# Where patch loads stand in the SyncE queue, and where GpSimd clears its buffers: one change to a fused token and transformer kernel

## What is computed

```python
pe   = conv(x, conv_w, stride 14)            # per image 9 x 9 patches, 256 channels
red  = mean of each 3 x 3 window of pe       # 9 windows per image
q    = ln(red) @ la_wq                       # 8 heads of 32
k, v = ln(window's 9 cells) @ la_wkv
agg  = softmax(q . k) weighted sum of v      # over the 9 cells of the window
lo   = red + agg @ la_proj_w + la_proj_b
patch_out = lo @ mod_w + mod_b               # 9 tokens
cls_out   = class attention over lo          # 1 token
h = concat(patch_out, cls_out, txt)          # 64 x 87 x 256
h = h + attention(ln(h))                     # 16 heads of 16, q and k normalised and rotated
h = h + ffn(ln(h))                           # linear + 2 of 8 low-rank experts
```

## Time and profile before

| | us |
|---|---|
| runs | 786.54, 795.9, 793.22 |
| median | 793.22 |
| the profiled execution's own time | 798.07 |
| its span, first to last instruction | 796.4 |

### The profile page before, as it was taken

The page is one execution under the profiler, slowest core; times in us unless marked ns, Lnnn a source line. Parts: engine busy times, 40 slices in busy tenths (PEclk is TensorE's granted clock), DMA queues, the critical chain, the costliest instruction groups (busy, mean ns, idle before and its releaser), DMA issues.

```text
span 796.4 us, 23804 instructions
## 1 busy us (share of the span) xinstructions
PE 708.1 (89%) x9335; PEld 564.9 (71%) x9335; DVE 547.5 (69%) x1208; ACT 408.2 (51%) x985; POOL 423.4 (53%) x450
## 2 busy tenths in 40 slices
PE   5998979987896388999899999999999999999974
PEld 4987757876673266887777777777777777877752
DVE  2377665873877556688677687887887887875641
ACT  4453423623433145666566556656557557666530
POOL 3577442652645726556447457566566566565211
PEclk9999969989897589999999999999999999999995
DMA  9940640704020121211221221222222222121100
GB/s 223 240 110 1 194 131 1 194 17 96 10 58 18 25 53 32 68 49 39 62 73 40 58 70 49 61 67 56 61 61 61 61 52 71 26 52 37 44 19 25
DMA packets 69524, 53.02 MB, mean 67 GB/s; under 512 B 36175, under 2 KB 68646, under 8 KB 69286
## 3 DMA queue, kind: packets, MB, share of 16 engines
q1 hardware_dynamic: 69414, 51.50, 25.9%
HBM read 33.69 MB, written 11.40 MB: 57 GB/s over the span
## 4 chain that ended last, share of the span: by engine, by line
PE 50%; DMA 13%; SPq 12%; DVE 11%; issue 5%; ACT 4%; POOL 4%; DVEq 0%; POOLq 0%; ACTq 0%
DMA out<-out_sb 8%; PE p_c L1305 8%; PE p_a L1305 7%; PE p_conv L764 6%; PE p_kv L764 6%; DMA xcols<-in_x_cols 5%; PE p_s L1366 4%; SPq L1060 4%; SPq L1061 4%; PE p_o L1375 3%; SPq L1050 2%; PE p_n L1383 2%; PE p_c L1423 2%; PE p_s L1348 2%; PE p_mm L764 2%
## 5 line engine op out<-in xcount | busy, mean ns | idle before, releaser
L1100 POOL TENSOR_TENSOR t<-t,ss_rs 116x512 f32<-116x512 f32 x48 | 51.0, 1062 | 152.8 <-ACT ss_rs L1149 152.8
L1243 DVE TENSOR_REDUCE mx<-p_s 87x16 bf16<-87x1392 f32 x64 | 102.2, 1597 | 8.9 <-PE p_s L1348 8.4
L1174 ACT ACTIVATE prT<-p_s 87x1392 f32<-87x1392 f32 x64 | 85.0, 1328 | 31.2 <-PE p_s L1366 31.2
L426 POOL TENSOR_TENSOR xs_lo<-xcols,xs_hi 120x585 fp32r<-120x585 f32 (+1 forms) x45 | 60.5, 1352 | 66.2 <-ACT xs_hi L489 66.2
L1096 POOL TENSOR_TENSOR t<-t 116x512 f32<-116x512 f32 x48 | 61.7, 1285 | 42.0 <-DVE t L1234 41.9
L1366 PE MATMUL p_s<-qr,kr 32*87 32x87 f32 x2048 | 68.6, 257 | 0.0
L1103 POOL TENSOR_TENSOR t<-t,tabs 116x512 f32<-116x512 f32 x48 | 61.1, 1273 | 1.5
L1305 PE MATMUL p_c<-w_f,yT 128*116 128x296 f32 x192 | 59.7, 436 | 1.7 <-ACT f L1199 0.6
L1366 PEld LDWEIGHTS p_s<-qr,kr 32*87 32x87 f32 x2048 | 60.1, 153 | 0.0
L1362 PE MATMUL p_s<-mxT,pick_row 32*87 32x87 bf16 x1024 | 55.7, 207 | 1.0 <-ACT mxT L1168 1.0
L1305 PE MATMUL p_c<-w_p,onT 128*116 128x256 f32 x192 | 54.3, 406 | 1.2 <-ACT yT L1193 0.9
(11 more groups left out here) (248 smaller groups left out, 1974.8 us busy)
## 6 DMA issues: line engine op xcount, KB each, us to landing
xcols<-in_x_cols SPq DMA_DIRECT2D x12, 822.7 KB, 11.8
h<-h_tokens SPq DMA_DIRECT2D x16, 348.0 KB
out<-out_sb SPq DMA_DIRECT2D x48, 116.0 KB
h_tokens<-in_txt SPq DMA_DIRECT2D x4, 1232.0 KB, 11.7
x<-in_txt_cols SPq DMA_DIRECT2D x32, 154.0 KB, 2.9
qr<-qkT SPq DMA_DIRECT2D x64, 58.0 KB, 2.0
kr<-qkT SPq DMA_DIRECT2D x64, 58.0 KB, 2.0
xcols<-in_x_cols SPq DMA_DIRECT2D x3, 759.4 KB, 13.5
```

The costliest lines, as they stand in the source:

```text
L426: nc.gpsimd.tensor_tensor(xs.lo[:, n % XS_SLOTS, :, 0:M].bitcast(F32R), raw, xs.hi[:, n % XS_SLOTS, :, 0:M], ALU.subtract).then_inc(S['xs_ ...
L1100: link(nc.gpsimd.tensor_tensor(t4, t4, ss_rs[:, b].unsqueeze(2).broadcast_to([TP, 2 * HEADS, HD]), ALU.mult))
L1174: nc.scalar.activation(prT[:, k % 2], p_s[0:SEQ, :, 0:QUADS * SEQ], ACT.Exp, scale=HD ** -0.5).then_inc(S['s_exp'], 1)
L1243: nc.vector.reduce_max(mx[:, k % 2, :, 0:QUADS], p_s[0:SEQ, :, 0:QUADS * SP].rearrange("p j (a k) -> p j a k", k=SP)[:, :, :, 0:SEQ], AX_X ...
```

## The change

Three edits. In SyncE's table `x.1` and `x.2` move from -64 and -30 to -317 and -245. In VectorE's table `sum.0` moves from 593 to 620. In GpSimd's code `clear()` is cut in two: the strips and `mx` are filled behind `xc` of group 1, `vp` behind the first `add` of group 0; the waits for the window stage's semaphores go with them.

```diff
--- before.py
+++ after.py
@@ -255,7 +255,7 @@
 WINDOW_DVE = table("""stats.0.-10 stats.1.48 xlo.0.55 stats.2.89 xlo.1.105 xlo.2.110 stats.3.147 xlo.3.162 xlo.4.172 stats.4.176
                 stats.5.183 stats.6.224 xlo.5.231 xlo.6.257 stats.7.304 stats.8.310 red_var.0.331 xlo.7.338
                 redb.0.342 xlo.8.375 q.0.380 q_kb.0.384 prod.0.400 score.0.427 prod.1.437 score.1.467 prod.2.477
-                score.2.498 s_max.0.517 att.0.538 sum.0.593 sum.1.638 lo.0.695 lo_var.0.700 patch.0.730 gv.0.752
+                score.2.498 s_max.0.517 att.0.538 sum.0.620 sum.1.638 lo.0.695 lo_var.0.700 patch.0.730 gv.0.752
                 g_m.0.774 g_att.0.818 gw.0.866 cls.0.960""")
 WINDOW_PE = table("""conv.0.-55 conv.1.-26 conv.2.6 xT.0.24 xT.1.41 conv.3.45 xT.2.63 conv.4.72 kv.0.90 xT.3.120 xT.4.122 conv.5.125
                 kv.1.143 kv.2.158 conv.6.172 xT.5.190 kv.3.193 conv.7.207 conv.8.225 xT.6.243 kv.4.246 kv.5.263
@@ -263,7 +263,7 @@
                 mod.0.718 patT.0.736 gv.0.738 gT.0.769 gB.0.850 ga.0.872 cl.0.910""")
 WINDOW_POOL = table("""xlo.0.-120 xlo.1.-71 xlo.2.-39 xlo.3.2 xlo.4.16 red.1.31 red.2.40 xlo.5.86 red.3.101 red.4.110 xlo.6.118
                 xlo.7.133 xlo.8.194 red.5.209 red.6.221 red.7.258 red.8.275 vw.0.551 vw.1.566 vw.2.582""")
-WINDOW_SP = table("""x.0.-398 x.1.-64 x.2.-30 rows.0.736 cls.0.970""")
+WINDOW_SP = table("""x.0.-398 x.1.-317 x.2.-245 rows.0.736 cls.0.970""")
 WINDOW_PERIOD = 403
 PIECES = CELLS // LOAD_CELLS
 X_SLOTS, XS_SLOTS, PE_SLOTS, XT_SLOTS, KV_SLOTS = 3, 3, 4, 3, 6
@@ -404,7 +404,7 @@
 
             return step
 
-        def gpsimd(pool, link, clear):
+        def gpsimd(pool, link):
             consts.fill_early(nc, pool, link)
             nc.gpsimd.memset(eps_q[:], 1e-5 * CELLS * CELLS * C).then_inc(S['fill'], 1)
 
@@ -449,12 +449,6 @@
                     if s == 0 and k == 2:
                         fill_pick()
                         consts.fill_late(nc, pool, link)
-                    if s == STEPS - 1 and k == 0:
-                        pool.wait_ge(S['conv'], CELLS * STEPS)
-                        pool.wait_ge(S['kv_mm'], CELLS * STEPS)
-                        pool.wait_ge(S['stat'], CELLS * STEPS)
-                        pool.wait_ge(S['red'], (CELLS - 1) * STEPS)
-                        clear()
 
             return step
 
@@ -1068,10 +1062,17 @@
         def gpsimd(pool, link):
             ready = counted(pool, S['set_0'])
 
-            def clear():
-
+            def clear_strips():
+
+                pool.wait_ge(W['conv'], CONVS)
                 for part in (qr, kr, mx):
                     ready(nc.gpsimd.memset(part[:], 0.0))
+
+            def clear_values():
+
+                pool.wait_ge(W['kv_mm'], CONVS)
+                pool.wait_ge(W['stat'], CONVS)
+                pool.wait_ge(W['red'], (CELLS - 1) * STEPS)
                 ready(nc.gpsimd.memset(vp[:, :, :, :, HD:], 1.0))
 
             def step(name, g, k):
@@ -1087,6 +1088,8 @@
                         "p c (b s) -> p c b s", b=GB))
                     nc.gpsimd.tensor_copy(images(x[:, half])[:, :, :, WINDOWS], consts.clsT[:, :, GB * g:GB * (g + 1)]
                                           ).then_inc(S['x_ok'], 1)
+                    if g == 1:
+                        clear_strips()
                 if name == 'xlo':
                     wait(pool, S['xhi'], g + 1)
                     nc.gpsimd.tensor_tensor(xT.lo[:, half].bitcast(F32R), x[:, half], xT.hi[:, half],
@@ -1094,6 +1097,8 @@
                 if name == 'add':
                     wait(pool, S['rot_ok'], 3 * g + k + 1)
                     link(nc.gpsimd.tensor_tensor(t1[:, b], t1[:, b], t2[:, b], ALU.add))
+                    if g == 0 and k == 0:
+                        clear_values()
                 if name == 'scale':
                     wait(pool, S['ss_rstd'], 3 * g + k + 1)
                     t4 = t1[:, b].rearrange("p (h d) -> p h d", d=HD)
@@ -1119,7 +1124,7 @@
                     link(nc.gpsimd.tensor_tensor(g_eq[:], g_eq[:], earlier[:].unsqueeze(1).broadcast_to(shape), ALU.mult))
                     nc.gpsimd.tensor_tensor(g_gt[:], g_gt[:], g_eq[:], ALU.add).then_inc(S['rank_in'], 1)
 
-            return step, clear
+            return step
 
         def scalar(act, link):
             def step(name, g, k):
@@ -1448,8 +1453,7 @@
         @block.gpsimd
         def _(pool):
             link = counted(pool, consts.S['pool_1'])
-            group_step, clear = groups[1](pool, link)
-            play(WINDOW_POOL, windows[1](pool, link, clear), GROUP_POOL, group_step)
+            play(WINDOW_POOL, windows[1](pool, link), GROUP_POOL, groups[1](pool, link))
 
         @block.scalar
         def _(act):
```

## The result

| | before | after |
|---|---|---|
| median of the timed runs, us | 790.55 (11 runs) | 767.94 (6 runs) |
| ratio, 95% interval | | 0.971 [0.966, 0.976] |
| profiled execution, us | 798.07 | 764.59 |
| its span, us | 796.4 | 762.9 |

The times are those of a second timing of both kernels, on one chip; the first gave 0.9705 [0.9628, 0.9783] with 767.93 us for the kernel after. So the gain is 22.9 us, with an interval from 19 to 27. A ratio leaves out the executions that ran slow (two of before and two of `sum_only` further down), a median takes all, so a gain worked out from a ratio can differ from the distance of two medians.

The account below looks back on a forecast made before the run. TensorE bounds the unchanged group stage, so the gain is in when that stage starts. Loads 10.5 us plus fills and sum 8.7 make 19.2, taking 793.2 to 774 us; range 765 to 785.

Parts of the forecast that it names:

- The fills and the sum: Between the stages: moved fills and `sum.0` behind `rotate.2` let `qk.0` of group 1 go 8.7 us earlier, bounds 7.8 to 9.4.
- `sum.0` within a microsecond behind `rotate.2`: Sign of being right, in the last step on VectorE: `sum.0` starts within a microsecond behind `rotate.2`.
- The third late load: Load `x.1` of step 4, at 187 us behind a row store: 9.2 us, from TensorE's 7.66 us wait plus 1.5 of clock.
- The rival by which it is shorter in other executions: Holes shorter in the timed runs: loads give 2.5 us, the whole 11.2, so 782 us; chance 0.12.
- The second late load: Load `x.1` of step 3, at 141 us behind a row store: 0.5 us, between 0 and ScalarE's idle 2.61.
- No such row of TensorE stands behind the second: Claim that no wait of TensorE follows the load at 141 us, though ScalarE sat idle 2.61 us.
- The share of 0.80 in 3.83: TensorE's wait against ScalarE's idle time at the load at 86 us, used to put the 141 us load at 0.5 us.
- The first late load: Load `x.1` of step 2, at 86 us behind a row store: 0.8 us, between nothing and ScalarE's 3.8.
- The cover "with only 0.2 us in hand": GpSimd's moved strips and `mx` fills end at 241.0 us, against 241.19 when the `add` begins, so they cost nothing.
- the first rival: Between the stages, fills slow VectorE or come late for `add.0`: 4.9 us lost, gain 14.3, so 779 us; chance 0.12.
- TensorE's clock as a loss: Rival: closer packed start keeps TensorE's clock low into the group stage; 30 us lost against 19 won, 804 us; chance 0.03.
- The first peak product some 19 us earlier: Sign of being right: the first peak product starts some 19 us earlier.

Follow-up runs that it names:

- `sum_only`: The kernel before with only `sum.0` put behind `rotate.2`, fills and loads as they were: ratio 0.9982, median 790.7 us.
- the kernel with copies: The kernel after with its two long GpSimd fills made by copies from one zero per partition: ratio 0.9671, 765.9 us.

## Why the prediction was nearly right

It said 774 us, 765 to 785; the time is 768, at the edge of the 768 to 778 that it gave its own working. The sum of 19.2 us came out as 22.9. Of the 6 us between 774 and 768 another 2.6 are luck of the starting point and no mechanism: the three runs of before that it started from had a median of 793.2, and with more runs it is 790.6. By the row stores, over all kernels, the terms 0.8, 0.5, 9.2 and 8.7 came out as 1.2, 4.8, 9.4 and 9.3, 24.7 together, inside the interval of the timed gain. So one term was wrong by far, and the total is near because the two large terms were right.

- **The fills and the sum, 8.7 us.** Measured 8.3 (5.1 to 11.5). The steps of that chain hold one by one: `sum.0` within a microsecond behind `rotate.2`, a wait for `qkT.1` of 4.76 us where about 5 were named, the bias held up by `add.2` (1.38 us), no product of VectorE over 2 us beside a fill.
- **The third late load, 9.2 us, 7.66 of wait and 1.5 of clock.** Measured by itself: 9.7 us by the row stores, 7.2 of wait and 2.3 of clock in its trace, 10.1 in the timed runs. The rival by which it is shorter in other executions falls: the 3rd row store stands 47.9 to 48.4 us ahead of the 4th in all four kernels with old loads.
- **The second late load, 0.5 us and at most 2.61: the step that failed.** It is worth 4.7 us by the row stores (3.2 by the median). "No such row of TensorE stands behind the second" was looked for right behind the load; the row stands 15 us on, as a wait for VectorE (2.67 us at 162.43 in the trace of before), with the clock's share behind it, which I had put down for the third load alone. Nor is ScalarE's idle time an upper bound: of some 2.5 us, 1.1 were left on GpSimd, VectorE's meeting with GpSimd made 2.0 of them, and the clock behind TensorE's wait doubled that. The share of 0.80 in 3.83, taken from the first load, had nothing to do with this path.
- **The first late load, 0.8 us.** 1.2 to 1.7 by the row stores, nothing in the timed runs: within the bounds.
- **The cover "with only 0.2 us in hand".** The row was read rightly, its meaning not. 4.4 us more of lateness showed no cost, for the idle time further down GpSimd's queue takes most of it up. That weakens the first rival's half on a late first `add`; the half on fills that hold VectorE up is out by the rows beside them.
- **TensorE's clock as a loss.** The clock is at nine tenths or more in every slice from the 15th on, but for the last, so that rival is out. "The first peak product some 19 us earlier" came 26.1 us earlier in these two traces (281.22 to 255.09), about what the four intervals between the row stores gained, their share of clock included.
- **A reading.** TensorE isn't at nine tenths in every slice from the 17th on, as was said: the 20th is an 8. Nothing hangs on it.

Open in part is the stage behind the fifth row store. Its work is the same in all kernels, and it took 505.7 to 515.4 us. Of the 10.6 us that the two profiled executions stand further apart than the medians, 7.7 lie there. A good part of the spread lies at the very end, in the stretch from TensorE's last group of products with `w_p` to the end of the span, where short waits follow one another. It took 21.4 to 25.9 us: 21.4 to 22.8 where the clock was granted at 0.74 to 0.79 on average, and 24.6 to 25.9 where it was 0.50 to 0.54. Before has 25.0 us of it, at 0.53, and after 22.7, at 0.74. Further up the executions differ in single stretches of low clock, such as 0.85 from 391 to 401 us in before. Whether the clock falls early or late in that last stretch differs between executions, with 22.68 us in both traces of the kernel after; what decides it was not tried.

## What to carry to other kernels

A wait on an engine that isn't the bottleneck is priced where its lateness arrives at the bottleneck, which may be some 15 us on and under another name; follow it down the queues before putting it at nothing. Count the bottleneck's low clock behind each wait too: here it was 2.1 us behind a wait of 2.7, and 1.7 to 2.3 behind one of over 7. A cover is all the idle time between the added work and the next thing that is truly waited for, not the first gap. Taking one wait away pays only if the next one behind it goes too. And when whole runs differ by a per cent, distances between marks that every step has show in which step the time moved.

## What the runs showed of the hardware

A fill holds the end of one kind of operation up after all. `epsb`, an addition and multiplication on three columns with one input in SBUF (`TENSOR_SCALAR`), began at 223.98 beside the second fill, and ended at 224.79, just behind the fill's end at 224.77; it took 0.81 us, and 0.15 and 0.16 us in the kernel with copies and in the kernel before, where GpSimd stood still at that time. It is 0.80 or 0.81 us in all ten traces that have a fill there. The two-input operations beside the same fill kept their length (0.42 and 0.95 us). It cost nothing here: VectorE's next operation began 0.08 us behind `epsb`, as without a fill, and took 0.73 us instead of 0.68. The Trainium skill (SBUF — State Buffer, Who interferes with whom) has `tensor_scalar` among the operations that can contend with GpSimd, in a mode that takes both ports and when their operands suit it; whether this one ran in that mode no run shows. I had read the section for the two-input operations only. What a long one-input operation beside fills would have cost was not tried.
